# Batch attention of a two-layer block: projections computed two groups ahead of the scores, with q in two buffers

## The reference, cut to what matters

```python
h = _layernorm(x, axis=-1) * (1 + cb) + sb
def _mha(x, Wqkv, bqkv, Wo, bo):           # D = 128, H = 4, hd = 32
    S, B, _ = x.shape
    qkv = x @ Wqkv.T + bqkv
    q, k, v = jnp.split(qkv, 3, axis=-1)
    q, k, v = (to_heads(q), to_heads(k), to_heads(v))
    scores = jnp.einsum('bhqd,bhkd->bhqk', q, k) * (1.0 / np.sqrt(hd))
    att = jax.nn.softmax(scores, axis=-1)
    o = jnp.einsum('bhqk,bhkd->bhqd', att, v)
    return o.transpose(2, 0, 1, 3).reshape(S, B, D) @ Wo.T + bo
y = _layer_norm(x + _mha(x, Wqkv, bqkv, Wo, bo), g1, be1)   # then the experts
```

## Time and profile before

| | |
|---|---|
| median of 3 runs | 1167.25 us (1165.15 to 1167.34) |
| profiled execution | 1176.8 us, of it span 1175.0 us |
| mean granted TensorE clock | 0.895 of full speed |
| busy over the span | PE 81%, DVE 77%, POOL 67%, ACT 55% |
| stage of the change | 705 to 877 us, about 15% of the span |

### The profile page before, as it was taken

One profiled execution on the slowest core, in us unless ns is written; L12 is line 12 of the kernel. 1 busy time (PEld: TensorE's weight loads), 2 busy tenths in 40 slices (PEclk: granted clock), 3 DMA queues, 4 the chain that ended last, 5 costly groups with the idle time before them and its releaser, 6 DMA issues. The chain is left out here.

```text
span 1175.0 us, 25297 instructions
## 1 busy us (share of the span) xinstructions
PE 950.1 (81%) x5489; PEld 689.5 (59%) x5489; DVE 901.3 (77%) x2728; ACT 640.5 (55%) x1626; POOL 790.2 (67%) x656
## 2 busy tenths in 40 slices
PE   3799999999778688888988953788858687989884
PEld 2565555555446455555555532556648587888773
DVE  2589999999949769888888966486656595777765
ACT  1555555444279556676677533676528205756652
POOL 0288888888712179999999957678706204777776
PEclk9899999999979889999999985799955557989997
DMA  7320000000000220000000005234423103333331
GB/s 217 102 88 1 0 0 0 0 0 0 1 1 0 81 64 18 9 18 18 9 18 18 10 27 153 67 95 105 106 69 103 50 1 91 99 99 102 102 100 45
DMA packets 67118, 61.25 MB, mean 52 GB/s; under 512 B 7812, under 2 KB 54096, under 8 KB 67042
## 3 DMA queue, kind: packets, MB, share of 16 engines
q1 hardware_dynamic: 58978, 41.47, 12.7%
q0 software_dynamic: 6912, 18.36, 5.4%
q10 hardware_dynamic: 1152, 0.52, 0.2%
HBM read 30.97 MB, written 21.50 MB: 45 GB/s over the span
## 5 line engine op out<-in xcount | busy, mean ns | idle before, releaser
L462 PE MATMUL a_pS<-a_kv,utri 128*128 128x360 f32 (+3 forms) x768 | 264.8, 481 | 19.4 <-issue 6.5
L453 POOL TENSOR_TENSOR a_kv<-a_qk,a_vv 128x1152 f32<-128x1152 f32 (+1 forms) x128 | 264.1, 2064 | 13.2 <-DVE a_qk L427 13.2
L558 POOL TENSOR_TENSOR a_tt<-a_tt 128x576 f32<-128x576 f32 (+1 forms) x128 | 157.0, 1227 | 64.1 <-DVE a_tt L542 64.0
L462 PEld LDWEIGHTS a_pS<-a_kv,utri 128*128 128x128 f32 x768 | 136.3, 191 | 100.6 <-DVE a_tt L542 30.5
L542 DVE TENSOR_TENSOR a_tt<-a_pS,a_qk 128x360 f32<-128x360 f32 (+3 forms) x384 | 180.8, 525 | 15.5 <-PE a_pS L462 8.5
L1761 POOL DMA_INDIRECT x_yl<-ys,e_row x72 | 70.5, 979 | 80.5 <-POOLq L1472 54.2
L570 DVE TENSOR_REDUCE a_nd<-a_tt 128x144 f32<-128x720 f32 (+3 forms) x128 | 104.2, 814 | 0.0
L508 ACT ACTIVATE a_tt<-a_pI 128x144 f32<-128x144 f32 (+1 forms) x96 | 40.1, 417 | 111.7 <-PE a_pI L470 111.7
L1707 PE MATMUL x_pZ<-w,x_hT 128*128 x576 | 82.0, 287 | 12.1 <-issue 8.9
L501 PEld LDWEIGHTS a_pO<-wgate,a_yT 128*128 128x128 f32 x256 | 42.8, 194 | 81.1 <-issue 51.8
L1767 POOL DMA_INDIRECT out_dram<-x_o,e_row_z x72 | 74.2, 1031 | 22.5 <-issue 21.1
(11 more groups left out here) (260 smaller groups left out, 2445.1 us busy)
## 6 DMA issues: line engine op xcount, KB each, us to landing
ys<-gw SPq DMA_DIRECT2D x16, 256.0 KB, 3.7
xs<-X SPq DMA_DIRECT2D x16, 256.0 KB, 2.3
X<-xs SPq DMA_DIRECT2D x16, 256.0 KB, 5.5
m_kx<-m_kc SPq DMA_DIRECT2D x64, 64.0 KB, 2.0
ys<-X SPq DMA_DIRECT2D x16, 256.0 KB, 2.9
m_ax<-m_pc SPq DMA_DIRECT2D x64, 64.0 KB, 2.0
ys<-U SPq DMA_DIRECT2D x16, 256.0 KB
w<-in_L_ffn_W_dram SPq DMA_DIRECT2D x1, 2048.0 KB
```

What stands on the lines that cost most here:

```text
L453: pool.tensor_tensor(kv[:, t % 2, :, :, :], kk.unsqueeze(2).to_broadcast([P, H, J, D]), vv[:, t, :, :].unsqueeze(3).to_broadcast([P, H, J, ...
L462: pe.matmul(pS[c][:, 0:(h1 - h0) * SC], K.utri[:, :], flat[:, h0 * SC:h1 * SC], start=True, stop=True).then_inc(u_done, 1)
L558: pool.tensor_tensor(tt[:, t % 2, :, :, D // 2:D], tt[:, t % 2, :, :, D // 2:D], tt[:, t % 2, :, :, 0:D // 2], ALU.add).then_inc(half_done, 1)
```

## The change

All projections move one step earlier relative to the scores. PE's step s now does scores(s), q/k/v(s+2), values(s-2), transposes(s+3), out(s-2). ACT does v(s+1), q(s+2), k(s+2), xn(s+4), o(s-2), hT(s+3), exp(s). POOL does h3 and xb(s+3), shift(s), h(s+4). SP issues kx(s+2), ax(s-1), rows(s+1). DVE's step function is unchanged. The loop starts at s = -4, one step earlier, and the statistics of x move one step earlier with it. qT has two buffers, and `act_q(g)` waits for the scores of group g-2 in place of g-1. The number of instructions of each kind stays.

```diff
-        hT, qT = sb("hT", [P, 4 * P]), sb("qT", [P, 4 * P])
+        hT, qT = sb("hT", [P, 4 * P]), sb("qT", [P, 2, 4 * P])
...
-        PARTS = [(-3, 0, 1), (-2, 1, 2), (-1, 2, 4), (0, 4, 6), (2, 6, 10), (5, 10, 16)]
-        x_groups = {-3: [0], -2: [1], -1: [2, 3], 0: [4, 5], 1: [6, 7], 2: [8, 9], 3: [10, 11], 4: [12, 13], 5: [14, 15]}
+        PARTS = [(-4, 0, 1), (-3, 1, 2), (-2, 2, 4), (-1, 4, 6), (1, 6, 10), (4, 10, 16)]
+        x_groups = {-4: [0], -3: [1], -2: [2, 3], -1: [4, 5], 0: [6, 7], 1: [8, 9], 2: [10, 11], 3: [12, 13], 4: [14, 15]}
...
         def act_q(act, g):
             act.wait_ge(q_ps, g + 1)
-            wait(act, s_ps, g)
-            act.activation(qT[:, :], pq[:, :], ACT.Identity, bias=K.cols[:, BQ:BQ + 1]).then_inc(q_ready, 1)
+            wait(act, s_ps, g - 1)
+            act.activation(qT[:, g % 2, :], pq[:, :], ACT.Identity, bias=K.cols[:, BQ:BQ + 1]).then_inc(q_ready, 1)
...
         def pe_step(pe, s):
             if there(s):
                 pe_scores(pe, s)
-            if there(s + 1):
-                pe_qk(pe, s + 1)
-                pe_v(pe, s + 1)
+            if there(s + 2):
+                pe_qk(pe, s + 2)
+                pe_v(pe, s + 2)
             if there(s - 2):
                 pe_values(pe, s - 2)
-            if there(s + 2):
-                pe_T(pe, s + 2)
+            if there(s + 3):
+                pe_T(pe, s + 3)
             if there(s - 2):
                 pe_out(pe, s - 2)
 
         def act_step(act, s):
-            if there(s):
-                act_v(act, s)
             if there(s + 1):
-                act_q(act, s + 1)
-                act_k(act, s + 1)
-            if there(s + 3):
-                act_xn(act, s + 3)
+                act_v(act, s + 1)
+            if there(s + 2):
+                act_q(act, s + 2)
+                act_k(act, s + 2)
+            if there(s + 4):
+                act_xn(act, s + 4)
             if there(s - 2):
                 act_o(act, s - 2)
-            if there(s + 2):
-                act_hT(act, s + 2)
+            if there(s + 3):
+                act_hT(act, s + 3)
             if there(s):
                 act_exp(act, s)
...
         def pool_step(pool, s):
-            if there(s + 2):
-                pool_h3(pool, s + 2)
-                pool_xb(pool, s + 2)
+            if there(s + 3):
+                pool_h3(pool, s + 3)
+                pool_xb(pool, s + 3)
             if there(s):
                 pool_shift(pool, s)
-            if there(s + 3):
-                pool_h(pool, s + 3)
+            if there(s + 4):
+                pool_h(pool, s + 4)
 
         def run(e, step, before={}):
 
-            for s in range(-3, G + 3):
+            for s in range(-4, G + 3):
...
                 def sp_step(sp, s):
-                    if there(s + 1):
-                        sp_kx(sp, s + 1)
+                    if there(s + 2):
+                        sp_kx(sp, s + 2)
                     if there(s - 1):
                         sp_ax(sp, s - 1)
-                    if there(s):
-                        sp_rows(sp, s)
+                    if there(s + 1):
+                        sp_rows(sp, s + 1)
```

More of the change, by code:

```diff
@@ L1144, in pe_scores @@
                     mm = pe.matmul(pS[32 * c:32 * c + 32, t * P:(t + 1) * P].rearrange("p (h s) -> p h s", h=FH),
-                                   qT[:, at:at + 32], kx[:, g % 2, :, at:at + 32], start=True, stop=True,
+                                   qT[:, g % 2, at:at + 32], kx[:, g % 2, :, at:at + 32], start=True, stop=True,
                                    skip_group_check=True)
```

## The result

| | median | ratio to before |
|---|---|---|
| before | 1167.3 us (4 runs) | |
| changed kernel | 1158.83 us (1155.31 to 1159.42, 4 runs) | 0.9923, interval 0.9899 to 0.9948 |
| changed kernel, run again | 1159.43 us (6 runs) | 0.9927, interval 0.9899 to 0.9954 |

The forecast was 1153.0 us, a gain of 14.2; measured is a gain of 8.5 us. The time lies inside the stated range of 1147.5 to 1160.5, but above the 1148 to 1156 of the forecast itself and above the 1157.6 to which the ends of its pieces reached. So the two profiles differ by twice what the medians do, and that was the first thing to explain.

What follows compares the result with a forecast made beforehand. A 7.68 us loop through the kx DMAs was taken to bound each step. Five pieces gave 14.2 us, 1175.0 to 1160.8 in the profiled span; the same gain from the 1167.25 median gave 1153.0 us, range 1147.5 to 1160.5.

Steps and rivals of the forecast that it cites:

- 1, start to scores(3): Up to scores(3): gain 4.2 us, the middle between 5.7 at PE's higher clock and 2.7 at the lower.
- 2, scores(3) to (6): Stretch with the large part of statistics, now 25.31 us: gain 1.0 us; 1.9 by the walk, less for a clock loss.
- 3, scores(6) to (14): Eight steady steps go from 7.65 to 6.87 us each: gain 6.3 us, between 6.1 and 6.9.
- 4, scores(14) to (15): Step 14, now 8.84 us, then without projections, takes 6.2 to 8.0 us: gain 1.8 us, between 0.8 and 2.7.
- 5, scores(15) to the end: Last stretch of the stage, now 19.66 us, same chain with less queued on PE: gain 0.9 us, between 0 and 2.
- The loop through kx and its removal: Scores, q, k, k copy, four kx issues and a landing hold each step at 7.68 us; PE's 0.73 us wait goes.
- The next bound: Steady steps afterwards: out, scores, q, k on PE and k, xn, o on ACT take 6.87 us; POOL just under, 6.69.
- ax early by 0.6 us: Steady steps: ax lands 10.1 us after its step's scores, and the next step's values need it at 10.69.
- The first rival: Steady steps held by ax or POOL near 7.2 us instead of 6.87: 1155.6 to 1158 us, chance 15%.
- The start and its waits: First steps: scores(0) come 2.5 to 3.5 us later; PE waits for v 3.8 us in step 1, 2.2 in step 4.
- The slower rival: New PE gaps in steps 1 and 4 lower its clock, 11.3 us a step: 4 us slower, 1171 us, chance 4%.
- The rival of longer statistics: Two later statistics parts: POOL stretches two more DVE operations in each from 0.19 to 1.19 us, 4 us lost: 1157, chance 7%.

Runs made afterwards that it cites:

- before_kx3: The kernel before with three of the four kx DMAs, head 3's keys never spread: 1219.36 us in a single run, beside 1234.77 for before on another chip.
- ax_fill: ax_first with extra matmuls, three in step 1 between k and v and one, two, one ahead of the values of groups 13, 14, 15: ratio to before 0.9882.
- ax_first: The changed kernel with the ax DMAs of a step issued ahead of its kx DMAs on SP: 1155.15 us, ratio to before 0.9884.
- ax_xn: ax_first with ACT doing the normalisation xn(s+4) ahead of the q and k copies in its step: ratio to before 0.9864.

## Why the prediction was right or wrong

The stage cut at the same scores matmuls, in us of gain. The stage's own start is the first statistics operation, since the profiles differ by up to 3.6 us ahead of it. All columns are single executions of before against the first profile of the changed kernel.

| piece | forecast | first profile of before | second profile of before |
|---|---|---|---|
| 1, start to scores(3) | 4.2 | 5.4 | 1.7 |
| 2, scores(3) to (6) | 1.0 | 1.1 | 1.0 |
| 3, scores(6) to (14) | 6.3 | 4.7 | 5.1 |
| 4, scores(14) to (15) | 1.8 | 2.1 | 1.0 |
| 5, scores(15) to the end | 0.9 | 1.1 | -1.2 |
| sum | 14.2 | 14.5 | 7.6 |

- **The loop through kx and its removal: right**, and shown by before_kx3 and by the missing wait in the changed kernel. That the sum of the loop met 7.68 exactly was no evidence: its last term of 0.1 us is what was left over. The evidence is that one issue less takes 0.6 us.
- **The next bound, 6.87 us by out, scores, q, k, xn, o: right**, 6.88 in the steps without disturbance, 6.84 on average with ax first, 6.70 with xn taken out of the loop.
- **ax early by 0.6 us: right as a median, wrong as a claim on all steps.** The first rival had it, at 15%, and it came about in part: piece 3 lost 1.6 us of its 6.3 against the same profile, to slow issues and landings (of the ax issued from 796.40 on, landings took 2.7 us in the median and up to 3.2). I had summed with the median issue and landing although a slow issue of kx(15) stood in the earlier trace rows. A margin of 0.6 us against a term that is 1 us longer now and then is no margin.
- **Pieces 4 and 5 and most of piece 1: the step that failed.** I measured the gain against one execution that was 9.5 us above the median of its own runs, noted the difference, and took the gain over unchanged. The second profile of before shows what was special in the first: the scores, q and k of all of steps 0 to 2 and everything from scores(15) on at the lower clock (a granted clock of 0.5, that is 1.2 GHz), where the second has the upper one in step 1 and in part of the rest, and a slow issue of kx(15). Against the second profile, which lies with the median, those three pieces are worth 1.5 us and not 6.9. That is why the forecast for the median was 5.8 us too low.
- **That the sum met the first profile within 0.3 us is partly luck.** Piece 1 gave 1.2 us more and piece 3 1.6 less than forecast. For piece 1 I had walked two ways, 5.7 us of gain at the higher clock and 2.7 at the lower, and took the middle; the walk at the higher clock is what happened, scores(2) at 33.89 and scores(3) at 43.04 us after the stage's start where it had 33.9 and 42.8. And that the measured 1158.8 us lie inside the range owes more to the room left for the rivals than to the sum, whose own low end was 1157.6. Its other end is added up wrongly: the upper ends of the pieces give 19.2, not 19.4.
- **The start and its waits: right.** scores(0) come 19.73 us after the stage's start, not 17.54 (2.2 later, forecast 2.5); v is awaited in step 1 for 3.71 us (forecast 3.8) and in step 4 for 2.19 (forecast 2.2). These are the two rows, beside the last of the earlier trace rows:

```profile
740.94 1.27 PE L1108 MATMUL m_pv<-W,m_hT 128*128 128x128 f32 x8 [3.71 <-ACT m_v L1134]
...
764.29 1.16 PE L1108 MATMUL m_pv<-W,m_hT 128*128 128x128 f32 x8 [2.19 <-ACT m_v L1134]
```

- **Piece 5 turned negative** against the second profile. In both executions PE ran at the lower clock for part of the last steps, but in the changed kernel for longer, up to the values of group 15. Of the 1.2 us, 0.86 are these values, first in the changed kernel, then in the second profile of before:

```profile
852.68 1.94 PE L1204 MATMUL m_pO<-m_ax,m_v 128*32 128x128 f32 x32
```

```profile
861.18 1.08 PE L1204 MATMUL m_pO<-m_ax,m_v 128*32 128x128 f32 x32 [1.05 <-DMA m_ax<-m_pc]
```

- **The slower rival did not come about.** The gap of 3.71 us was followed by scores at the lower clock (743.00, 1.94 us) and k at the upper again, the one of 2.19 us by values and out of 1.64 and 1.69 us and then by scores at the upper one. So the clock fell as the rival says; but it came back each time before PE had done one round of its matmuls, and ax_fill shows that for the gap in step 1 it cost nothing. The rival's price of 11.3 us for a step at the lower clock was not sound either: the 7.30 us of the earlier trace rows come from a window with a mean clock of 0.67, in which v and the transposes ran faster.
- **The rival of longer statistics did not cost what it named.** In the last two parts of the statistics six operations took 0.97 us or more in the changed kernel, four in the first profile of before and seven in the second, and the two waits for v came as forecast.
- **The rule of the Trainium skill** on the ports that DVE and POOL share ("SBUF — State Buffer", the section on the two separate sides) showed itself in another operation than the one I weighed. The product `vec_probs` has two SBUF inputs, and takes 0.68 us where it does not start during a POOL operation. Its row in step 8 of the first profile of before, and in step 7 of the changed kernel:

```profile
804.24 0.97 DVE L1178 TENSOR_TENSOR m_pn<-m_ex,m_rc 128x512 f32<-128x512 f32 x1
```

```profile
785.75 1.71 DVE L1178 TENSOR_TENSOR m_pn<-m_ex,m_rc 128x512 f32<-128x512 f32 x1
```

POOL in step 7 of the changed kernel, xb and then the softmax shift:

```profile
785.63 1.28 POOL L1077 TENSOR_TENSOR X<-X,m_gb 128x512 f32<-128x512 f32 x1
786.85 1.51 POOL L1083 TENSOR_TENSOR m_s<-m_sm,m_mx 128x512 f32<-128x512 f32 x1
```

In both kernels `vec_probs` begins while POOL is in xb and ends 0.55 us after xb does (805.21 against 804.66, 787.46 against 786.91); in the changed kernel it begins earlier within xb, and so waits longer. POOL then waits in its turn: the shift takes 1.04 to 1.05 us where no `vec_probs` runs, 1.42 to 1.52 where it begins during one, and it ends 0.90 to 0.92 us after `vec_probs` each time. Both directions agree with the rule, up to a small head start: the one that comes second ends as if it had begun 0.13 to 0.14 us before the other's end. DVE has the time for it: ax_first has the same 1.7 us and steps of 6.84 on average. POOL has less: the shift's wait of some 0.45 us is part of the 6.69 us that I took for POOL's own work, and of the 6.70 us at which ax_xn stands, where POOL has no idle time left. No run takes it out.

## What to carry to other kernels

When an engine waits for "issue" in every step, look in the DMA queue for the landing that ends just then. Here a lead of one step and a spare buffer removed it, and the DMAs that have become the later ones then belong first in the queue. Before summing a gain piece by piece against one profiled execution, compare it with the median of its runs: if it is as far off as the gain itself, every piece at the ends of a stage has to be priced from a second profile or given a range that reaches to nothing. A stop in which two engines wait for each other cost less here while the pipeline was still filling than one step later (a stage of 149.10 against 152.38 us).

## What the runs showed of the hardware

- PE's granted clock after a gap is not the same from one execution to the next. After gaps of 3.0 us the scores ran at the lower level (1.93 us) in the first profile of before, after gaps of 3.4 and 3.3 us at the upper (1.08 us) in the second; behind the latter it was q and k that ran at the lower level (2.04 and 1.85 us). Shorter gaps were followed by the lower level too: 2.38 us in before_kx3 (scores of 1.94 us) and 2.07 us at scores(15). What decides between them stays open.
- An issue of kx or ax on SP takes 0.59 us in the median, and single ones up to 1.8 us, in both kernels; landings take 2.0 us in the median and up to 4.0. In the two profiles of before none of the 128 ax issues took over 0.61 us, in the changed kernel they took up to 1.75. No run here tells what makes the slow ones.
- A DVE product with two SBUF inputs and a POOL operation that reads SBUF do not run side by side: in all profiles of this case `vec_probs` ended 0.54 to 0.56 us after the POOL operation during which it had started (save where that one was within 0.02 us of its end), and the shift 0.90 to 0.92 us after the `vec_probs` during which it had started. Alone they take 0.68 and 1.05 us.
- The same kernel took 1167 us on one chip and 1230 to 1235 us on another, with the stage of the change nearly equal (156.61, and 158.76 for the kernel with q's buffer alone).
